# Routing of a mixture of experts taken off VectorE in a chunk pipeline beside two LSTMs

## The reference

```python
x = x + attn0(lstm_a(x))          # LSTM, then linear attention with ReLU features
y = rnn_c(x)                      # tanh RNN
x = x + ffn0(y)                   # 8 heads of 32 features, 16 experts, the best 2 of each head
# second layer: lstm_e, attention with layer norm, gated RNN, 8 experts of which 4
```

```python
logits = t @ expert_emb           # t: 32 features of a head, 16 logits
w = softmax(logits)
topw, topi = top_k(w, 2)
out = sum over the two experts of topw * (gelu(t @ W1[e] + b1[e]) @ W2[e] + b2[e])
```

## Time and profile before

| what | value |
|---|---|
| median of 3 runs | 2672.86 us (2663.55 to 2673.28) |
| the profiled execution | 2674.83 us, its span 2672.8 us |
| mean granted TensorE clock | 0.945 |
| TensorE matmul, busy | 2434.5 us, 91% of the span |
| TensorE weight loads, busy | 2042.9 us, 76% |
| VectorE, busy | 1876.5 us, 70% |
| ScalarE, busy | 1143.1 us, 43% |
| GpSimd, busy | 397.3 us, 15% |
| first stage, transposes L1075 | 324, from 29.8 to 1362.5 us |

### The profile page before, as it was taken

The page is one execution under the profiler, slowest core; times in us unless marked ns, Lnnn a source line. Parts: engine busy times, 40 slices in busy tenths (PEclk is TensorE's granted clock), DMA queues, the critical chain, the costliest instruction groups (busy, mean ns, idle before and its releaser), DMA issues. The chain is left out here.

```text
span 2672.8 us, 119359 instructions
## 1 busy us (share of the span) xinstructions
PE 2434.5 (91%) x50848; PEld 2042.9 (76%) x50848; DVE 1876.5 (70%) x7416; ACT 1143.1 (43%) x3693; POOL 397.3 (15%) x412
## 2 busy tenths in 40 slices
PE   4779999999999999998768869999999999999999
PEld 2556777777777777764546669999999999999998
DVE  4667777777777777788456666767667767776674
ACT  3226555555555555567247633333333333333332
POOL 0000000000000000000039502222222222222222
PEclk8679999999999999999669869999999999999999
DMA  6000000000000000101014220000000000000000
GB/s 187 2 2 3 6 5 5 5 6 5 5 5 5 6 5 5 37 13 28 3 51 124 78 81 7 9 9 9 9 9 9 9 9 9 9 9 9 5 5 6
DMA packets 53195, 53.68 MB, mean 20 GB/s; under 512 B 25126, under 2 KB 47288, under 8 KB 50746
## 3 DMA queue, kind: packets, MB, share of 16 engines
q1 hardware_dynamic: 47878, 30.57, 4.1%
q0 software_dynamic: 1728, 12.58, 1.4%
q10 hardware_dynamic: 3060, 2.90, 0.4%
HBM read 39.46 MB, written 6.57 MB: 17 GB/s over the span
## 5 line engine op out<-in xcount | busy, mean ns | idle before, releaser
L105 PE MATMUL p<-xn,m_h 128*128 128x128 f16 x6144 | 557.7, 219 | 0.0
L105 PE MATMUL p<-xn,m_l 128*128 128x128 f16 x3072 | 529.0, 219 | 0.0
L105 PEld LDWEIGHTS p<-xn,m_h 128*128 128x128 f16 x6144 | 479.8, 98 | 1.8
L2157 POOL TENSOR_TENSOR xn<-qkv_w,xn 128x384 f16<-128x384 f32 x256 | 233.8, 913 | 896.2 <-ACT xn L2115 896.2
L612 PE MATMUL lg_b<-xn,lh 128*32 128x256 f16 x6144 | 299.5, 290 | 63.9 <-DVE lh L1105 56.2
L891 ACT ACTIVATE hm<-xy,b 128x512 f32<-128x512 f32 x512 | 347.5, 679 | 0.0
L874 ACT ACTIVATE gl<-gt 128x128 f32<-128x128 f32 (+1 forms) x324 | 93.0, 287 | 566.9 <-DVE gt L1075 566.9
L1075 DVE STREAM_TRANSPOSE gt<-lg_b 128x512 f32<-128x512 f32 (+1 forms) x324 | 193.6, 598 | 190.7 <-PE lg_b L612 190.2
L105 PEld LDWEIGHTS p<-xn,m_l 128*128 128x128 f16 x3072 | 300.5, 98 | 0.7
L2041 PE MATMUL po<-m_h,xn 128*128 128x256 f16 x1536 | 293.3, 272 | 1.9 <-DVE xn L2196 1.9
L612 PEld LDWEIGHTS lg_b<-xn,lh 128*32 128x32 f16 x6144 | 160.8, 101 | 145.8 <-DVE lh L1105 102.6
(11 more groups left out here) (392 smaller groups left out, 6197.4 us busy)
## 6 DMA issues: line engine op xcount, KB each, us to landing
m_stage<-in_m_w POOLq DMA_DIRECT2D x12, 1024.0 KB, 5.2
hs<-in_m_w SPq DMA_DIRECT2D x16, 384.0 KB, 3.2
x_dram<-x SPq DMA_DIRECT2D x16, 128.0 KB, 2.1
xs<-in_l_wv SPq DMA_DIRECT2D x1, 2048.0 KB
attention_dram<-att SPq DMA_DIRECT2D x16, 128.0 KB, 2.8
xn<-x_dram SPq DMA_DIRECT2D x16, 128.0 KB, 2.5
xn<-attention_dram SPq DMA_DIRECT2D x128, 16.0 KB, 1.8
out_dram<-xn SPq DMA_DIRECT2D x16, 128.0 KB, 2.2
```

The costliest lines, as they stand in the source:

```text
L105: ins = pe.matmul(out, w[wp](k), x[xp](k), start=start, stop=last and k == KT - 1 and xp == 1, skip_group_check=True)
L2157: pool.tensor_tensor(a_l[:, n % 2, :], a32[:, n % 2, :], a_h[:, n % 2, :], ALU.subtract).then_inc(a_lo, 1)
```

## The change

In slot 11 the scaling of the logits from PSUM moves from VectorE to ScalarE (`logits`, between the RNN's tanh and the second gelu). The subtraction of the maximum moves to GpSimd. The eight index searches, all in slot 12 before, are split into four in slot 11 and four in slot 12. The half tanh moves on ScalarE from the end of slot 12 to its start, ahead of the gate tanh. The cast of the indices and the making of the mask move from VectorE to GpSimd and ScalarE: GpSimd casts, subtracts both places from the expert numbers, multiplies the two differences and squares the product, and ScalarE takes relu(1 - square), which is 1 at the two places and 0 elsewhere. The reciprocal of 1 - t moves from slot 13 to slot 12. In slot 15 the scaling of `acc` to `om_h` moves from VectorE to ScalarE.

```diff
-        ROUTE = 2 * NH + 11
-        rest_p = sem("rest_p")
-        CHOSEN = 2 * NH + 2
+        ROUTE = 2 * NH + 6
+        FOUND = 2 * NH
+        below, rest_p, chosen, mask_done = (sem(n) for n in ("below", "rest_p", "chosen", "mask_done"))
...
-                elif slot == 12 and routes(i):
-                    act.wait_ge(route, ROUTE * (i - 2) + NH + 1)
-                    act.activation(rt[:, 1, :, :], rt[:, 0, :, :], ACT.Tanh, scale=0.5).then_inc(route_t, 1)
-                elif slot == 15 and routes(i):
+                if slot == 13 and routes(i):
+                    act.wait_ge(chosen, 5 * (i - 1))
+                    act.activation(rt[:, 2, :, :], rt[:, 3, :, :], ACT.Relu, scale=-1.0, bias=1.0).then_inc(mask_done, 1)
+                if slot == 15 and nth("sum", i, slot, N_E) is not None:
+
+                    act.wait_ge(acc_done, nth("sum", i, slot, N_E) + 1)
+                    act.activation(om_h[:, :, :], acc[:, :, :], ACT.Copy, scale=1.0 / S).then_inc(om_hi, 1)
+                if slot == 15 and routes(i):
...
+            def logits(i):
+
+                act.wait_ge(z_full, Z_AT[i, 11] + 1)
+                if i > 2:
+                    act.wait_ge(route, ROUTE * (i - 2))
+                act.activation(lg[:, :, :].rearrange("p h e -> p (h e)"), z[:, 0:NH * E1], ACT.Copy,
+                               scale=1.0 / S).then_inc(z_free, 1)
+
+            def half_tanh(i):
+
+                act.wait_ge(below, i - 1)
+                act.activation(rt[:, 1, :, :], rt[:, 0, :, :], ACT.Tanh, scale=0.5).then_inc(route_t, 1)
...
+                if slot == 12 and routes(i):
+                    half_tanh(i)
                 gates(i, slot)
                 gelu(i, slot, 0)
                 cell_tanh(i, slot)
                 rnn_tanh(i, slot)
+                if slot == 11 and routes(i):
+                    logits(i)
                 gelu(i, slot, 1)
...
+                if slot == 11 and routes(i):
+
+                    pool.wait_ge(route, ROUTE * (i - 2) + NH)
+                    pool.tensor_tensor(rt[:, 0, :, :], lg[:, :, :], m8[:, :, 0].unsqueeze(2).to_broadcast([P, NH, E1]),
+                                       ALU.subtract).then_inc(below, 1)
                 if slot == 12 and routes(i):
 
                     pool.wait_ge(route_t, i - 1)
                     pool.tensor_scalar(rt[:, 4, :, :], rt[:, 1, :, :], -1.0, 1.0, ALU.mult, ALU.add).then_inc(rest_p, 1)
+                    pool.wait_ge(route, ROUTE * (i - 2) + FOUND)
+                    pool.tensor_copy(idf[:, :, :], i8[:, :, 0:2]).then_inc(chosen, 1)
+                    pool.wait_ge(chosen, 5 * (i - 2) + 1)
+                    io = iota[:, :].unsqueeze(1).to_broadcast([P, NH, E1])
+                    for j in range(2):
+                        pool.tensor_tensor(rt[:, 2 + j, :, :], io, idf[:, :, j].unsqueeze(2).to_broadcast([P, NH, E1]),
+                                           ALU.subtract).then_inc(chosen, 1)
+                    pool.wait_ge(chosen, 5 * (i - 2) + 3)
+                    pool.tensor_tensor(rt[:, 2, :, :], rt[:, 2, :, :], rt[:, 3, :, :], ALU.mult).then_inc(chosen, 1)
+                    pool.wait_ge(chosen, 5 * (i - 2) + 4)
+                    pool.tensor_tensor(rt[:, 3, :, :], rt[:, 2, :, :], rt[:, 2, :, :], ALU.mult).then_inc(chosen, 1)
...
                 if slot == 11:
-                    dve.wait_ge(z_full, Z_AT[i, slot] + 1)
-                    dve.tensor_scalar(lg[:, :, :].rearrange("p h e -> p (h e)"), z[:, 0:NH * E1], 1.0 / S, None,
-                                      ALU.mult).then_inc(z_free, 1)
                     dve.wait_ge(z_free, Z_AT[i, slot] + 1)
                     for h in range(NH):
                         dve.max(m8[:, h, :], lg[:, h, :]).then_inc(route, 1)
                     dve.wait_ge(route, r + NH)
-                    dve.tensor_tensor(rt[:, 0, :, :], lg[:, :, :], m8[:, :, 0].unsqueeze(2).to_broadcast([P, NH, E1]),
-                                      ALU.subtract).then_inc(route, 1)
+                    for h in range(NH // 2):
+                        dve.max_index(i8[:, h, :], m8[:, h, :], lg[:, h, :]).then_inc(route, 1)
                 elif slot == 12:
 
-                    for h in range(NH):
+                    for h in range(NH // 2, NH):
                         dve.max_index(i8[:, h, :], m8[:, h, :], lg[:, h, :]).then_inc(route, 1)
-                    dve.wait_ge(route, r + 2 * NH + 1)
-                    dve.tensor_copy(idf[:, :, :], i8[:, :, 0:2]).then_inc(route, 1)
-                    dve.wait_ge(route, r + CHOSEN)
-                    io = iota[:, :].unsqueeze(1).to_broadcast([P, NH, E1])
-                    for j in range(2):
-                        dve.tensor_tensor(rt[:, 2 + j, :, :], io, idf[:, :, j].unsqueeze(2).to_broadcast([P, NH, E1]),
-                                          ALU.is_equal).then_inc(route, 1)
-                    dve.wait_ge(route, r + CHOSEN + 2)
-                    dve.tensor_tensor(rt[:, 2, :, :], rt[:, 2, :, :], rt[:, 3, :, :], ALU.add).then_inc(route, 1)
-                elif slot == 13:
-
                     dve.wait_ge(rest_p, i - 1)
                     dve.reciprocal(rt[:, 5, :, :], rt[:, 4, :, :]).then_inc(route, 1)
-                    dve.wait_ge(route, r + CHOSEN + 4)
+                elif slot == 13:
+
+                    dve.wait_ge(route, r + FOUND + 1)
                     dve.scalar_tensor_tensor(out=rt[:, 6, :, :], in0=rt[:, 1, :, :], scalar=1.0, in1=rt[:, 5, :, :],
                                              op0=ALU.add, op1=ALU.mult).then_inc(route, 1)
-                    dve.wait_ge(route, r + CHOSEN + 5)
+                    dve.wait_ge(route, r + FOUND + 2)
                     dve.tensor_reduce(sm[:, 0, :], rt[:, 6, :, :], AX_X, ALU.add).then_inc(route, 1)
+                    dve.wait_ge(mask_done, i - 1)
                     dve.tensor_tensor(rt[:, 7, :, :], rt[:, 6, :, :], rt[:, 2, :, :], ALU.mult).then_inc(route, 1)
...
                 elif slot == 15 and nth("sum", i, slot, N_E) is not None:
 
-                    dve.wait_ge(acc_done, nth("sum", i, slot, N_E) + 1)
-                    dve.tensor_scalar(om_h[:, :, :], acc[:, :, :], 1.0 / S, None, ALU.mult).then_inc(om_hi, 1)
                     dve.wait_ge(om_hi, i - 2)
```

More of the change, by code:

```diff
@@ L1204, in routing @@
                                              op0=ALU.add, op1=ALU.mult).then_inc(route, 1)
-                    dve.wait_ge(route, r + CHOSEN + 5)
+                    dve.wait_ge(route, r + FOUND + 2)
                     dve.tensor_reduce(sm[:, 0, :], rt[:, 6, :, :], AX_X, ALU.add).then_inc(route, 1)
+                    dve.wait_ge(mask_done, i - 1)
                     dve.tensor_tensor(rt[:, 7, :, :], rt[:, 6, :, :], rt[:, 2, :, :], ALU.mult).then_inc(route, 1)
-                    dve.wait_ge(route, r + CHOSEN + 7)
+                    dve.wait_ge(route, r + FOUND + 4)
@@ L1209, in routing @@
                     dve.reciprocal(sm[:, 1, :], sm[:, 0, :]).then_inc(route, 1)
-                    dve.wait_ge(route, r + CHOSEN + 8)
+                    dve.wait_ge(route, r + FOUND + 5)
                     dve.tensor_tensor(wts[:, :, :], rt[:, 7, :, :], sm[:, 1, :].unsqueeze(2).to_broadcast([P, NH, E1]),
```

## The result

| | before | after |
|---|---|---|
| median, measured in turns on one chip | 2673.07 us (2663.55 to 2677.89) | 2641.8 us (2639.94 to 2652.72) |
| ratio after / before | | 0.9896, 95% interval 0.9857 to 0.9934 |
| the profiled execution, its span | 2674.83, 2672.8 us | 2642.64, 2640.6 us |
| mean granted TensorE clock | 0.945 | 0.949 |
| a second measurement, another chip | 2676.15 us | 2643.3 us, ratio 0.9873 (0.9855 to 0.989) |

The change is faster by about 1%. So the sign, the mechanism and most of the size came as forecast, and more was gained than the working has terms for.

A forecast was written before the change was run, and what follows sets the result against it. VectorE's own work was taken to bound routing slots 12 and 13, with TensorE next in slot 14. 12 x (1.47 - 0.10) + 5.0 + 0.8 = 22.2 us, against the median 2672.86, gave 2651 us, range 2643 to 2666.

The forecast's parts named there:

- T12: Start of slot 12's transpose (T plus number: that slot's transpose); slot 11's moved work was to make it 0.06 us later.
- Slot 12: Four searches and the reciprocal on VectorE; slot to last 3.97 us instead of 4.73, next transpose 0.70 earlier.
- The hold: Two-input VectorE instruction in slot 13 finishes only after the GpSimd instruction in progress: 0 to 0.15 us per chunk, 0.10 taken.
- S14: Start of slot 14's recurrent matmuls (S plus number: that slot's); forecast 2.14 us after slot 13's transpose, before any hold.
- Rival C: Slower: a GpSimd product costs 1.3 us, not 0.42, delaying gates and mask; 0.95 us lost per chunk, 2688 us; chance 0.06.
- rival A: Half the gain: hold of 0.7 to 0.9 us per chunk from GpSimd's waits or integer copy; 2662 us; chance 0.19.
- The wait for the mask: Slot 13: VectorE's masked product waits 0.10 to 0.23 us for ScalarE's mask, which stands behind the spread copy.
- Slot 14 and TensorE: TensorE's 0.54 us wait for `wts` goes; its queue then sets slot 15's matmuls; slots 13 and 14 together 0.77 us shorter.
- the ring: Recurrent steps: matmuls to transpose at least 1.55 us, then gate tanh, cell and state to the next matmuls 2.14 us.
- Slot 15: Scaling of `acc` on ScalarE: worth nothing in chunks 4 to 15, because TensorE's projections bound slot 0.
- The short chunks: Chunks 2, 3, 16, 17: 1.24 us each after a 0.3 hold, 5.0 in all; plus 0.8 for slot 15 in chunks 16 to 18.
- Rival B: No gain: ScalarE's logits or TensorE's queue ahead of slot 14's matmuls takes the room; 2669 us; chance 0.11.

The follow-up runs named there:

- The two added products: Changed kernel with two idle GpSimd products of 128 columns behind its slot 12 block: slot 13 4.15 us in nine full chunks, 4.33 in three; median chunk 70.35.
- The earlier mask pass: Changed kernel with ScalarE's mask relu ahead of slot 13's second gelu instead of at the slot's end: chunk 70.11 us, one execution 2631.91 us.

## Why the prediction was right, step by step

**Slot 11, T12 0.06 later.** Measured 0.06 (3.84 against 3.78). ScalarE had the logits in time, and MAX8 and the four searches took what was added up for them.

**Slot 12, 3.97 us.** Measured 3.93 in chunk 9. From the start of the reciprocal to the transpose it is 0.85 (663.66 to 664.51), not 0.89: the transpose, which doesn't wait for it, starts 0.08 before its end. The half tanh was hidden with 0.5 us to spare, forecast 0.45.

**The hold, 0 to 0.15, taken 0.10.** Measured 0.14: S14 is T13 + 2.28 (664.51, 666.79) instead of 2.14. L1123 took 0.38 us for 0.19 and ended at 665.92, 0.05 behind GpSimd's end at 665.87. The rule drawn from the earlier trace rows held for another line, size and chunk. What the Trainium skill says of the shared SBUF interfaces (GPSIMD Engine Reference, "Key points") agrees with this trace (0.38 us beside GpSimd, 0.19 without it). The two added products then showed what the rule as I had stated it lacks: each two-input instruction is held by one GpSimd instruction at most and then has its turn, so the holds do not grow with the length of the block.

**GpSimd's block.** It ended 1.36 us after T13, forecast 1.3. (The prices of the prediction add up to 678.54 to 678.66, 1.34 to 1.46 after T13, not to the 678.45 to 678.6 that it gives; the slip is 0.06 to 0.09 us and moves nothing else.) Products took 0.40 to 0.46 us (forecast 0.40 to 0.43 from the earlier trace rows), the cast 0.20 (forecast 0.2). The Trainium skill's 2.6 cycles per element (GPSIMD Engine Reference, "Elementwise — side-by-side cycle accounting") gave an estimated 0.46; only L1093, the product of the two differences, comes to that, the others took 0.40 and 0.41. Rival C needed 1.0 us a product and is out, and so is rival A, whose hold of 0.7 to 0.9 us would have left slot 13 near 4.7.

**The wait for the mask, 0.10 to 0.23.** Measured 0.07: the multiply-add came at T13 + 2.63 (667.14), so the masked product could start at 3.16, and it started at 3.23. The earlier mask pass removed it and took 0.08 out of slot 13. So T14 is T13 + 4.00, inside 3.89 to 4.02 by two errors that cancel (hold larger, wait smaller).

**Slot 14 and TensorE.** Here is the one mechanism of the ring that I had slightly wrong. I had TensorE's own queue set S15, at T13 + 6.12, and slot 14 last about 3.8. The wait for `wts` went, as forecast, and L706 came 2.17 after S14, not 2.31. So TensorE was early, if only by some 0.03 us (the earlier mask pass let no more through), and S15 is T14 + 2.15 (668.51 to 670.66), set by the state: slot 14 stayed at 3.69. The prediction had named this path too, at T13 + 6.16; measured 6.15, hold and mask included. What it had wrong is that it took the hold off once more. Slots 13 and 14 together are 0.77 shorter, as forecast without the hold. This is the largest part of the difference per chunk, 0.09 of 0.13 (the other 0.04 is the earlier transpose of slot 13): 1.50 us measured, 1.37 forecast, over 12 chunks 1.6 us (in the sums 18.2 against 16.4).

**Slot 15.** Worth nothing in the full chunks: shown by the kernel with this part alone (71.65 against 71.64).

**The short chunks, 5.0 + 0.8.** Measured 8.2, the term most off in the ring. Slots 12 and 13 gave 6.6 of it where 5.0 was forecast: they were 0.80 to 1.15 and 0.71 to 0.83 shorter, and the hold there was 0.16, not 0.3. It fell on the cell update (L1128, 0.36 us for 0.17 in chunk 3), not on the gate product (0.20 for 0.17). Nothing came of the 0.8 for slot 15: outside slots 12 and 13 chunks 16 and 17 were 0.4 and 0.6 longer. Chunk 2 alone gained 4.1 us; there the granted clock was back at its upper level at 192.3 us instead of 202.3. In a second trace of the same changed kernel chunk 2 gained 2.6. So a part of this is clock as well.

**What the sum left out.** "The later stages get the same instructions at a shifted time" is where the prediction was blind. It priced chunk 19, which has no routing, at nothing. It gave 8.1 us here and 6.5 in the second trace of the change, from the granted clock. That this time does not follow the routing work is shown by the slot 15 kernel, which gains 14.8 us there although its full chunks last as long as before (71.65), and by the kernel with the reciprocal moved back, which gains nothing (88.7 us). Both traces of the changed kernel have it, so it is part of what the change is worth as measured; it comes by the clock and not by shorter work. What makes the clock fall earlier or later in chunk 19 for kernels so alike stays open. Such microseconds also decide whether the time is in the stated range (the first measurement by the ratio) or under it (the second); that part is luck. With chunk 19 evened out by idle matmuls in both kernels, the change is worth 27.2 us by the medians, 25.6 in chunks 2 to 17; the forecast of 22.2 is short by 3 to 5 us, 1.9 of them in the full chunks (18.3 against 16.4) and 1.5 in the short ones (7.3 against 5.8).

Rival B (no gain) fell with the first slot time. That the change came out clearly faster, where 0.29 had been given to no difference, owes something to the 8 us of clock as well: with 22 us and the same width of interval the ratio would have been 0.988 to 0.996, faster still, but with less room.

## What to carry to other kernels

Find the slots in which the engine's own queue sets the pace and those in which it waits, and move work from the first to the second: the reciprocal, made neither shorter nor fewer, gained 0.63 us a chunk by standing in slot 12 instead of slot 13, while 0.28 us taken off slot 15 gained nothing. When work goes to GpSimd beside VectorE, add to the sum one hold of at most a GpSimd instruction for each two-input VectorE instruction on the path that meets one, not the length of the block. And judge a change of 1% by the lengths of the stretches it touches; a total carries a scatter of 10 to 25 us here (2637.12 to 2648.44 us for the changed kernel on one chip, 2655.94 to 2680.49 for the one before on another), part of it from the granted clock.

## What the runs showed of the hardware

- **VectorE and GpSimd take turns.** A VectorE instruction with two SBUF inputs that starts while a GpSimd instruction runs ends 0.03 to 0.06 us after it (0.38, 0.28 and 0.35 us instead of 0.19), and GpSimd's instructions are stretched in turn (0.45 and 0.56 us instead of 0.40). Where both start within 0.02 us, either can go first (L1133 0.18 us in nine chunks, 0.43 in three). With two more products queued, the slot grew by 0.15 us in those nine and 0.33 in the three, and not by their 1.0.
- **The granted clock where TensorE has idle time.** In the opening and in chunk 19, where TensorE waits for the state in most slots (in the changed kernel it is busy for 99.4 of 130 us and for 56.1 of 78.5), the granted clock was 0.67 (60 to 190 us) and 0.54 to 0.79 (stretches of chunk 19 and the last slots). The same instructions of chunk 19 and the last four slots took from 71.9 to 88.7 us over the kernels that run them unchanged.
- **Idle matmuls can pay.** Five in each slot brought the window 60 to 190 us from 0.67 to 0.91, and both ends together 16 us of the whole, though they add work to the engine that is busiest.
- **A reciprocal is dear on VectorE.** 0.93 us for 128x128 in float32, where a product or a reduction of the same tile takes 0.29.
